# The input of two depthwise convolutions turned in 56-row tiles, with longer DMA runs

## The chip, the core and the metric

The kernel runs on one core of a Trainium2 chip. The metric is the device time of one execution in microseconds (us); the median of three runs counts.

## What is computed

A ConvNeXt block is followed by a second depthwise convolution, both in float32 over 16 images of 96 channels of 56x56 pixels.

```python
y = depthwise_conv7x7(x) + dw_b
y = layernorm_over_channels(y) * ln_w + ln_b
y = gelu(y @ w1 + b1)                                  # 96 -> 384
gx = sqrt(sum over pixels of y**2); nx = gx / (mean(gx) + 1e-6)
y = grn_gamma * (y * nx) + grn_beta + y
z = x + y @ w2 + b2                                    # 384 -> 96
out = depthwise_conv3x3(floor_to_2^-16(z), w_pow2) + bias_fixed
```

## The kernel before, in words

There are three stages, one after the other: the 7x7 convolution (`stages["a"]`, writes `y_scratch`), the two dense layers (writes `z_scratch`), and the 3x3 convolution (`stages["c"]`, writes the output). The change touches the two convolutions.

A convolution works on 24 batches of four channels (CB = 4), two batches to a loop body (parity p). Its contraction runs over 112 partitions, which are a pair of image rows (2 x 56 columns); weights are banded 112x128 tables, one set for each channel. For each batch the following happens, with `s` running over 0 to 3:

- SP loads the batch (`load_rows`, L341) into `xin`: 112 partitions are 2 images (even and odd) x 4 channels x 14 runs of four rows; in each partition lie 8 image pairs x 224 elements. Two DMAs of 56 partitions each. The tables follow (`load_tables`, L368).
- PE turns the input (`tin`, L593): each transpose takes 112 partitions x 112 elements (a row pair of 8 channel-images) and writes 112 partitions x 112 elements in PSUM. A group `s` is four transposes for four images; the two banks `p_in` alternate, so group n waits until group n-2 has been evicted. Groups of the next batch are turned ahead by the table `AHEAD`: groups 0 and 1 before channel 0, group 2 before channel 1, group 3 before channel 2.
- ACT copies each group to `xt_h` (rounded to fp32r, `xt_copy`, L745, two instructions of 112x224) and DVE makes the low part `xt_l` (`low_part`, L951, two instructions of 112x224).
- PE convolves channel `s` (`convolve`, L617): 12 matmuls of 464 columns in the 7x7 stage, 4 in the 3x3 stage, into one of two banks `p_conv`. It first waits until the channel two before has been evicted.
- The result is copied to `yt` in three instructions of 224 elements (`yt_copy`): ACT (L762) does it for all channels of the 7x7 stage and for channels 0 to 2 of the 3x3 stage, DVE (L1155) for channel 3 of the 3x3 stage.
- PE turns a quarter of the batch before back (`back`, L644): eight transposes of 56 partitions x 112 elements, alternately from the upper and the lower half of the partitions, each half into its own bank. The wait for the output buffer (`back_waits`) stands ahead of the last matmul of `convolve`.
- The turned rows are copied to `ost` by `out_copy`: ACT (L772) in the 7x7 stage, DVE (L1144) in the 3x3 stage. The 7x7 stage has one pair of banks for this (`p_back`), the 3x3 stage two pairs, which alternate. SP stores the batch in two DMAs of 56 partitions (L385), two batches later in the 7x7 stage and three in the 3x3 stage.

Each engine runs its list in the written order. On DVE in the 3x3 stage this is, for each `s`: `low_part` of the groups turned ahead, then at `s` = 3 the copy `yt_copy`, then `out_copy` of the batch before. In the 7x7 stage DVE runs `low_part` and then three instructions of the running mean and variance (`update`); ACT runs `xt_copy` with `table_high` (L780), then `yt_copy`, then `out_copy`.

## Time and profile before

| | |
|---|---|
| median of three runs | 1070.03 us (1067.22 to 1071.70) |
| profiled execution | 1071.91 us; its span 1070.1 us |
| PE busy | 992.1 us, 93% of the span |
| PE weight loads | 718.5 us, 67% |
| DVE busy | 822.0 us, 77% |
| ACT busy | 823.5 us, 77% |
| POOL busy | 415.4 us, 39% |
| DMA | 182.95 MB in 146788 packets, 140564 of them under 2 KB; mean 171 GB/s |

The 7x7 stage takes about the first 350 us, the dense layers run to about 870 us, the 3x3 stage takes the rest. Busy times of PE hold modelled ends of pipelined matmuls; starts are measured, so the cost of a group of PE instructions is read here from its start to the start of the next group.

### The profile page before, as it was taken

How to read it: one execution, taken by the hardware profiler on the slowest of the kernel's cores; microseconds unless marked ns; L12 is line 12 of the kernel's file. 1: busy time of each engine (PE TensorE's matmuls, PEld its weight loads, DVE VectorE, ACT ScalarE, POOL GpSimd, SP SyncE). 2: the span in 40 equal slices, each digit the busy share in tenths (PEclk: the TensorE clock that was granted, in tenths of full speed). 3: DMA queues.
4: the chain of work that ended last, by engine and by line, in shares of the span. 5: the costliest groups of instructions: out<-in, count | busy, mean ns of one | idle time of the engine just before them, and what ended most of it. 6: DMA issues, size and time to landing. Idle time of an engine off the chain costs nothing.

```text
span 1070.1 us, 21112 instructions
## 1 busy us (share of the span) xinstructions
PE 992.1 (93%) x5574; PEld 718.5 (67%) x5574; DVE 822.0 (77%) x1718; ACT 823.5 (77%) x1715; POOL 415.4 (39%) x357
## 2 busy tenths in 40 slices
PE   5999999999999378999999999999999869999996
PEld 4788888888888265666666666666666427777774
DVE  5777777777777567988888888888887767888885
ACT  3688888888887356789898888888888608787874
POOL 3576766766766145333233323333332001111110
PEclk9899999999999667999999999999999989999998
DMA  8377777777774492555555555555543347999995
GB/s 183 99 189 183 183 181 180 180 182 180 181 180 120 126 235 76 179 155 177 164 172 161 177 164 171 162 169 163 165 141 90 101 116 178 244 251 243 249 240 150
DMA packets 146788, 182.95 MB, mean 171 GB/s; under 512 B 13939, under 2 KB 140564, under 8 KB 143796
## 3 DMA queue, kind: packets, MB, share of 16 engines
q1 hardware_dynamic: 144020, 179.86, 62.8%
q10 hardware_dynamic: 2736, 2.72, 1.2%
q8 instruction: 13, 0.21, 0.1%
q14 instruction: 19, 0.16, 0.1%
HBM read 124.28 MB, written 58.25 MB: 171 GB/s over the span
## 4 chain that ended last, share of the span: by engine, by line
PE 70%; DVE 10%; ACT 7%; issue 5%; DMA 4%; SPq 1%; DVEq 1%; POOL 1%; ACTq 0%; POOLq 0%
PE psum L617 21%; PE psum L697 21%; PE psum L687 6%; PE psum L688 6%; PE psum L689 6%; PE psum L593 5%; PE psum L644 3%; DVE arena_r L951 3%; ACT arena L762 3%; ACT arena_r L745 2%; DVE arena L979 1%; DVE arena L975 1%; DMA arena<-lines_a 1%; ACT arena L850 1%; DVE arena L1155 1%
## 5 line engine op out<-in xcount | busy, mean ns | idle before, releaser
L617 PE MATMUL psum<-arena_r 112*128 112x464 f32 x1536 | 375.9, 386 | 3.5 <-DVE arena_r L951 3.3
L617 PEld LDWEIGHTS psum<-arena_r 112*128 112x128 f32 x1536 | 277.1, 190 | 36.7 <-issue 3.0
L697 PE MATMUL psum<-arena,w2s 128*96 128x448 f32 x672 | 269.2, 545 | 5.8 <-DVE psum L1072 3.0
L850 ACT ACTIVATE arena<-psum,b1g 128x448 f32<-128x448 f32 x336 | 201.7, 631 | 60.2 <-PE psum L689 60.2
L528 POOL TENSOR_TENSOR arena_r<-arena,arena_r 96x448 fp32r<-96x448 f32 x112 | 136.9, 1222 | 268.8 <-DVE arena_r L1025 212.2
L697 PEld LDWEIGHTS psum<-arena,w2s 128*96 128x96 f32 x672 | 110.4, 165 | 124.4 <-issue 112.9
L687 PE MATMUL psum<-arena_r,w1h 96*128 96x448 f32 x336 | 153.8, 458 | 16.1 <-POOL arena_r L528 16.1
L762 ACT ACTIVATE arena<-psum,bias_a 64x224 f32<-64x224 f32 (+1 forms) x288 | 117.3, 443 | 59.0 <-PE psum L617 48.9
L951 DVE TENSOR_TENSOR arena_r<-psum,arena_r 112x224 fp32r<-112x224 f32 x384 | 127.4, 382 | 42.9 <-ACT arena_r L745 42.2
L517 POOL TENSOR_TENSOR arena<-arena 128x448 f32<-128x448 f32 x96 | 110.3, 1149 | 111.6 <-DVE arena L979 111.0
L745 ACT ACTIVATE arena_r<-psum 112x224 fp32r<-112x224 f32 x384 | 112.7, 356 | 52.9 <-PE psum L593 51.6
L817 ACT ACTIVATE arena<-arena 128x1792 bf16<-128x1792 f32 (+1 forms) x91 | 136.8, 1503 | 2.7
L593 PE MATMUL psum<-ident,arena 112*112 112x112 f32 x768 | 107.5, 274 | 28.2 <-DVE arena_r L951 13.1
L502 POOL TENSOR_TENSOR arena_r<-arena,arena_r 112x512 fp32r<-112x512 f32 x96 | 123.2, 1297 | 15.2 <-ACT arena_r L780 15.2
L688 PE MATMUL psum<-arena_r,w1h 96*128 96x448 f32 x336 | 126.2, 376 | 0.0
L689 PE MATMUL psum<-arena_r,w1l 96*128 96x448 f32 x336 | 125.8, 375 | 0.0
L975 DVE TENSOR_TENSOR arena<-arena,psum 128x448 f32<-128x448 f32 x96 | 59.6, 621 | 82.7 <-ACT arena L762 82.7
L593 PEld LDWEIGHTS psum<-ident,arena 112*112 112x112 f32 x768 | 76.7, 137 | 41.9 <-DVE arena_r L951 21.6
L762 ACT ACTIVATE arena<-psum,bias_c 64x224 f32<-64x224 f32 (+1 forms) x216 | 88.1, 442 | 18.2 <-PE psum L617 16.4
L644 PEld LDWEIGHTS psum<-ident,arena 56*112 56x112 f32 x1536 | 57.5, 131 | 62.7 <-issue 57.7
L1072 DVE TENSOR_TENSOR psum<-arena,psum 96x448 f32<-96x448 f32 x112 | 69.6, 621 | 33.3 <-PE psum L697 32.9
L559 POOL CAST arena_r<-arena 112x1024 fp32r<-112x1024 bf16 x24 | 25.0, 1042 | 175.8 <-PE psum L617 159.9
(98 smaller groups left out, 1145.5 us busy)
## 6 DMA issues: line engine op xcount, KB each, us to landing
arena<-lines_a SPq DMA_DIRECT2D x46, 448.0 KB
arena<-in_x_dram SPq DMA_DIRECT2D x48, 392.0 KB
y_scratch<-arena SPq DMA_DIRECT2D x48, 392.0 KB
arena<-in_x_dram SPq DMA_DIRECT2D x112, 168.0 KB, 2.6
z_scratch<-arena SPq DMA_DIRECT2D x112, 168.0 KB, 2.0
out_dram<-arena SPq DMA_DIRECT2D x48, 392.0 KB
arena<-z_scratch SPq DMA_DIRECT2D x44, 392.0 KB
arena_r<-y_scratch SPq DMA_DIRECT2D x98, 168.0 KB, 2.6
```

The costliest lines, as they stand in the source:

```text
L528: pool.tensor_tensor(yl[:, CH * t:CH * t + CH], ct[:, (t + p) % 2, :], yh[:, CH * t:CH * t + CH].bitcast(F32), ALU.subtract).then_inc(yn_r ...
L593: mm = nc.tensor.transpose(p_in[s % 2][0:PAIR, at:at + CM], xin[:, p, IG // 2 * s + i, PAIR * h:PAIR * h + PAIR], ident[0:CM, 0:CM])
L617: mm = nc.tensor.matmul(p_conv[s % 2][:, 0:NCOL], w[:, p, s, TW * k:TW * k + TW], v[:, p, s, slot0 + k:slot0 + k + JP, :].rearrange("p j i ...
L687: nc.tensor.matmul(p_h[m][:, 0:CH], w1h[:, w], yh[:, cols], start=True, stop=False)
L688: nc.tensor.matmul(p_h[m][:, 0:CH], w1h[:, w], yl[:, cols], start=False, stop=False)
L689: nc.tensor.matmul(p_h[m][:, 0:CH], w1l[:, w], yh[:, cols], start=False, stop=True).then_inc(h_done, 1)
L697: mm = nc.tensor.matmul(p_o[k][0:C, 0:CH], w2s[:, p, m, :], hid[p][:, m, CH * t:CH * t + CH], start=(m == 0), stop=(m == MT - 1))
L745: ins = nc.scalar.activation(tile_group(xt_h, p, s, h), bank_group(s, h), ACT.Identity)
L762: ins = nc.scalar.activation(to[part, q], cols[part, :, :, j:j + 2 * NRUN - 1:2], ACT.Identity, bias=bias[part, bass.ds(n, 1)], scale=scale)
L817: nc.scalar.activation(sqd[:, 0:CH * (t1 - t0)], hid[p][:, m, CH * t0:CH * t1], ACT.Square, accum_out=ss[:, p, m, part:part + 1]).then_inc ...
L850: nc.scalar.activation(hid[p][:, m, CH * t:CH * t + CH], p_h[m][:, 0:CH], ACT.Gelu, bias=b1g[:, m:m + 1]).then_inc(gelu_done, 1)
L951: ins = dve.tensor_tensor(tile_group(xt_l, p, s, h), bank_group(s, h), tile_group(xt_h, p, s, h).bitcast(F32), ALU.subtract)
```

## The change

Rows are loaded and stored in runs of eight instead of four (RUN = 448 elements, 7 runs to an image). Four images instead of two lie in the partitions: on the load side two in partitions 0 to 55 and two in 64 to 119 (images of the first and of the second eight), on the store side all four in 0 to 111. A load or store of a batch is four DMAs of 28 partitions instead of two of 56; the bytes are the same and each contiguous piece is twice as long.

The input is turned in two halves `u` of a batch instead of four groups. A half is 16 transposes of 56 partitions x 112 elements, alternately from the lower and the upper half of the array, each into its own bank, so a half fills a pair of banks. `TURN` puts half 0 ahead of channel 0 and half 1 ahead of channel 2. The 7x7 stage has one such pair (`p_in["a"]`; its first batch also borrows the banks of `p_conv`), the 3x3 stage two. For this the 3x3 stage gives up the second pair of `p_back`: both stages now have one. The waits of `tin` are moved ahead of the last matmul of the convolution before it. `xt_copy` and `low_part` are four instructions for each half of a batch, still of 224 elements, and signal after every two.

The copy to `yt` is one instruction of 336 elements on 128 partitions and two of 112 on 64 partitions, instead of three of 224. `yt` has another order of pixels, with runs of 7 instead of 14 elements. The number of transposes back, their shape and the copies out of them stay as they were.

```diff
-RUN = 4 * W
-NRUN = H // 4
+RUN = 8 * W
+NRUN = H // 8
+RP = 4
-CM = 2 * CR
+CM = 4 * CR
+HM = 2 * CR
+TURN = ((0,), (), (1,), ())
+TURN0 = ((), (0,), (), (1,))
-        p_in, p_conv = bank[0:2], bank[2:4]
-        p_back = {"a": [psum[:, 4:6, :]], "c": [psum[:, 4:6, :], psum[:, 6:8, :]]}
+        p_conv, p_back = bank[2:4], psum[:, 4:6, :]
+        p_in = {"a": [psum[:, 0:2, :]], "c": [psum[:, 0:2, :], psum[:, 6:8, :]]}
...
+        def turned_back(s, p):
+            to = yt[:, p].rearrange("p q i (c m) -> p q c i m", c=CB)[:, :, s]
...
+            return ((to[:, 1:RP], odd[:, 0:RP - 1], slice(0, TW)), (to[low, 0], even[low, 0], low), (to[high, 0], odd[high, RP - 1], high))
...
-                for g in range(2):
-                    sp.dma_start(xin[CR * g:CR * g + CR, s, :, :], rows_of[g][bass.ds(b * CR, CR)]).then_inc(S[f"x{s}"], 16)
+                for g in range(4):
+                    sp.dma_start(xin[in_part(g), s, :, :], image_rows(src, g)[bass.ds(b * CR, CR)]).then_inc(S[f"x{s}"], 16)
...
-                    need(pe, S["xt"], n - 1)
-                    for h in range(2):
-                        for i in range(IG // 2):
-                            at = CM * (IG // 2 * h + i)
-                            mm = nc.tensor.transpose(p_in[s % 2][0:PAIR, at:at + CM],
-                                                     xin[:, p, IG // 2 * s + i, PAIR * h:PAIR * h + PAIR], ident[0:CM, 0:CM])
+                    need(pe, S["xt"], 4 * b + 2 * u - 2 * (len(p_in["a" if S is stages["a"] else "c"]) - 1))
...
+                    for h in range(RP):
+                        for i in range(2):
+                            at = HM * (2 * h + i)
+                            for half in range(2):
+                                q = LSTEP * half
+                                mm = nc.tensor.transpose(in_pair(S, b, u)[0:PAIR, half, at:at + HM],
+                                                         xin[q:q + HM, p, 2 * u + i, PAIR * h:PAIR * h + PAIR],
+                                                         ident[q:q + HM, q:q + HM])
...
-                        if then_back and n == len(todo) - 1:
-                            back_waits(b - 1, s)
+                        if n == len(todo) - 1:
+                            if then_back:
+                                back_waits(b - 1, s)
+                            for q in then_turn:
+                                tin_waits(*q)
...
-                    need(pe, S["out"], G * b + s + 1 - len(outs))
+                    need(pe, S["out"], G * b + s)
...
-                dve.tensor_copy(rows_group(p, s), forwards(p_back["c"][s % 2][0:CM], IG)).then_inc(S["out"], 1)
+                dve.tensor_copy(rows_group(p, s), forwards(p_back[0:CM], RP)).then_inc(S["out"], 1)
```

Ahead of the 3x3 stage the first two batches are loaded in two steps: what has been written of z so far, and then the last two images (`first_rows`). Before, three of the four groups to be turned rested on the first step alone; now one of the two halves does.

## Rows read from the trace of the kernel before

**Rows 1.** Windows: us, busy PE PEld DVE ACT POOL, clock, DMA share, GB/s.

```profile
200.00:300.00 100.00, 99.29 (x693) 81.34 (x692) 73.76 (x145) 81.64 (x201) 69.34 (x59) 1.00 0.73 182
600.00:840.00 240.00, 240.00 (x889) 155.94 (x888) 197.96 (x410) 212.98 (x334) 72.70 (x61) 1.00 0.51 152
950.00:1000.00 50.00, 47.43 (x432) 35.44 (x430) 40.96 (x101) 40.57 (x116) 6.55 (x7) 1.00 0.94 247
```

**Rows 2.** Timeline, PE in the 7x7 stage: start us, us, line, shapes.

```profile
203.67 0.43 PE L644 MATMUL psum<-ident,arena 56*112 56x56 f32 x8
204.03 0.98 PE L593 MATMUL psum<-ident,arena 112*112 112x112 f32 x8
204.78 2.77 PE L617 MATMUL psum<-arena_r 112*128 112x464 f32 x12
207.48 0.43 PE L644 MATMUL psum<-ident,arena 56*112 56x56 f32 x8
208.01 0.60 PE L593 MATMUL psum<-ident,arena 112*112 112x112 f32 x4
208.37 2.76 PE L617 MATMUL psum<-arena_r 112*128 112x464 f32 x12
```

**Rows 3.** Lines, the whole span: two copies out of PSUM on ACT.

```profile
L762 ACT ACTIVATE arena<-psum,bias_a 64x224 f32<-64x224 f32 (+1 forms) x288 | 117.3, 443 | 59.0 <-PE psum L617 48.9 <-DVE arena L979 8.8
...
L772 ACT ACTIVATE arena<-psum 112x448 f32<-112x448 f32 x96 | 52.5, 546 | 5.1 <-PE psum L644 2.9
```

**Rows 4.** Timeline, all engines, one batch of the 3x3 stage.

```profile
942.65 1.10 ACT L745 ACTIVATE arena_r<-psum 112x224 fp32r<-112x224 f32 x4 [0.88 <-PE psum L593]
...
942.68 1.09 PE L617 MATMUL psum<-arena_r 112*128 112x464 f32 x4
943.10 0.62 DVE L1144 COPY arena<-psum 112x448 f32<-112x448 f32 x1
...
943.70 0.42 PE L644 MATMUL psum<-ident,arena 56*112 56x56 f32 x8
943.75 1.28 DVE L951 TENSOR_TENSOR arena_r<-psum,arena_r 112x224 fp32r<-112x224 f32 x4
...
944.50 0.59 PE L593 MATMUL psum<-ident,arena 112*112 112x112 f32 x4 [0.37 <-DVE arena_r L951]
...
944.96 0.61 DVE L1144 COPY arena<-psum 112x448 f32<-112x448 f32 x1
...
947.05 1.36 SPq L341 DMA_DIRECT2D arena<-z_scratch  x2
...
949.01 0.42 PE L644 MATMUL psum<-ident,arena 56*112 56x56 f32 x8
949.24 1.27 DVE L1155 TENSOR_SCALAR arena<-psum,bias_c 128x224 f32<-128x224 f32 x3
```

**Rows 5.** Waits, the whole span (us in total, times, longest).

```profile
PE psum L593 <- DVE arena_r L951: 13.1, 25, 2.9
...
PE psum L593 <- DMA arena<-z_scratch: 3.1, 1, 3.1
```

**Rows 6.** DMA issues, the whole span.

```profile
out_dram<-arena SPq DMA_DIRECT2D x48, 392.0 KB
...
arena<-lines_c SPq DMA_DIRECT2D x48, 112.0 KB
```

**Rows 7.** Timeline, all engines, the last channels and the tail.

```profile
1056.50 0.42 PE L644 MATMUL psum<-ident,arena 56*112 56x56 f32 x8
...
1056.97 0.62 DVE L1144 COPY arena<-psum 112x448 f32<-112x448 f32 x1 [0.78 <-PE psum L644]
...
1061.40 0.96 PE L644 MATMUL psum<-ident,arena 56*112 56x56 f32 x16 [0.18 <-DVE arena L1144]
```

**Rows 8.** Windows: two half microseconds of the tail, stores alone.

```profile
1063.50:1064.00 0.50, 0.00 (x0) 0.00 (x0) 0.14 (x1) 0.00 (x0) 0.00 (x0) 0.58 0.82 168
...
1066.00:1066.50 0.50, 0.00 (x0) 0.00 (x0) 0.00 (x0) 0.00 (x0) 0.00 (x0) 0.50 0.96 326
```

More of the change, by code:

```diff
@@ L470, in _ @@
             for b in range(2):
-                first_rows(b, 0, NI2 - 1, c_early[b])
+                for g in range(4):
+                    first_rows(b, g, 0, NI - g // 2, c_early[b])
                 tables_c(b, b)
@@ L657, in body @@
                         for s in range(G):
+                            turns = TURN0 if first and p == 0 else TURN
                             if not (last and p == 1):
-                                for q in (AHEAD0 if first and p == 0 else AHEAD)[s]:
-                                    tin(b + 1, q, 1 - p)
-                            convolve(b, s, p, not (first and p == 0))
+                                for u in turns[s]:
+                                    tin(b + 1, u, 1 - p)
+                            then_turn = [(b + 1, u, 1 - p) for u in turns[s + 1]] if s + 1 < G else [(b + 2, u, p) for u in TURN[0]]
+                            if last and (p == 1 or s + 1 == G):
+                                then_turn = []
+                            convolve(b, s, p, not (first and p == 0), then_turn)
                             if not (first and p == 0):
@@ L736, in conv_stage, with xt_copy @@
             def conv_stage(S, bias, scale, rows_too):
-                def xt_copy(b, s, p):
-                    act.wait_ge(S["tin"], G * b + s + 1)
-                    if s == 0:
+                def xt_copy(b, u, p):
+                    act.wait_ge(S["tin"], 2 * b + u + 1)
+                    if u == 0:
                         need(act, S["conv"], CB * (b - 1))
-                    for h in range(2):
-                        ins = nc.scalar.activation(tile_group(xt_h, p, s, h), bank_group(s, h), ACT.Identity)
-                    ins.then_inc(S["xh"], 1)
+                    for half in range(2):
+                        for c in range(2):
+                            ins = nc.scalar.activation(turned(xt_h, p, u, half, c), in_bank(S, b, u, half, c), ACT.Identity)
+                        ins.then_inc(S["xh"], 1)
                 def yt_copy(b, s, p):
@@ L780, in table_high @@
                     nc.scalar.activation(toep_h[:, p, s, :], toep[:, p, s, :], ACT.Identity).then_inc(S["th"], 1)
-                for s in range(G):
-                    if rows_too and s == G - 1:
+                for u in range(2):
+                    if rows_too and u == 1:
                         table_high(0, 0, 0)
-                    xt_copy(0, s, 0)
+                    xt_copy(0, u, 0)
                 if rows_too:
@@ L963, in body @@
                             if not (last and p == 1):
-                                for q in (AHEAD0 if first and p == 0 else AHEAD)[s]:
-                                    low_part(S, b + 1, q, 1 - p)
+                                for u in (TURN0 if first and p == 0 else TURN)[s]:
+                                    low_part(S, b + 1, u, 1 - p)
                             update(b, s, p)
```

155 lines of the change are left out of this document (78 added, 77 removed).

## The prediction, made before the changed kernel was run

> **What bounds the kernel now.** The windows come first [rows 1]: in the 7x7 stage PE is busy 99.29 of 100 us, in the dense layers all the time (the change leaves these alone), in the 3x3 stage 47.43 of 50 us, there with the DMA engines busy 0.94 of the time. So the question in the first stage is what a turn costs on PE, in the third whether PE, DVE or the DMA sets the pace.
>
> The timelines answer it. In the 7x7 stage, start to start [rows 2]: eight 56x56 transposes back 0.36 us (203.67 to 204.03), eight 112x112 turns 0.75 (to 204.78), four turns 0.36, a channel of 12 matmuls 2.70 (to 207.48). The turn at 208.01 starts 0.17 later than 207.48 + 0.36. In the 3x3 stage [rows 4] a channel takes 1.02 us (942.68 to 943.70), the transposes back 0.36, and the turn at 944.50 starts 0.44 late, named as waiting for DVE. One batch is 2x0.36 + 0.75 = 1.47 of turns, 4x1.02 = 4.08 of matmuls, 4x0.36 = 1.44 of transposes back and 0.44 of wait: 7.43 us. So nothing but DVE holds PE in a batch. The waits agree [rows 5]: turns waited 13.1 us for L951, and for a DMA of z only once, 3.1 us.
>
> **Turns.** The new form, 56x112 with 56 moving columns, is the form of L644: 0.36 us for eight [rows 2], so 0.72 for a half of 16 and 1.44 for a batch, against 1.47. A pair in both halves of the array turns what one 112x112 tile turned and takes 0.09 us against 0.09. The turns themselves give 0.03 us a batch. The Trainium skill (TensorEngine Tiling (Array Packing), Theoretical Speedup) promises up to twice the speed where a dimension is at most 64; by that a half would cost 0.36. The row speaks against it, since L644 is already tiled so; it is a rival below.
>
> **7x7 stage.** The wait of 0.17 goes, as the pair has two channels (over 6 us) to be evicted. ACT then has, ahead of channel 0, four copies (1.10, [rows 4]), two tables of 512 columns (estimate 0.62 each, from L772's 546 ns for 448), 1.15 to `yt` and 0.55 out [rows 3], about 4.0 us against a slot of 3.78; the next slot has 1.1 us less work than it lasts, and the bank is not wanted again for over 2 us. So no wait follows. Gain: 0.20 a batch x 23 = -4.6. At the start both halves are turned without waiting for an eviction: estimate -1 (between 0 and -2).
>
> **Copy to `yt`.** Three of 224 become 336 + 112 + 112. From L762 (224: 443 ns) and L772 (448: 546 ns) [rows 3] a column costs between 0.46 ns (their difference, over 224 columns) and 1.4 (DVE's 0.62 us for 448, with nothing fixed [rows 4]). 112 columns fewer are 0.05 to 0.15 us; I take 0.1, so 1.15 for both engines. The shorter runs are not in the trace; bound: 0 to +10%.
>
> **3x3 stage: the second pair of output banks.** This is the term that decides. `back` of slot s may now start only when `out_copy` of s-1 has ended on DVE, and DVE runs `low_part` ahead of it. The hand over from PE to DVE takes 0.05 (1056.50 + 0.42 to 1056.97) and from DVE to PE 0.06 (1061.34 to 1061.40) [rows 7]; DVE's `yt` copy begins 0.23 after the `back` behind its channel (949.01 to 949.24); the last matmul of a channel starts 0.78 after the first, 0.24 ahead of `back` (four matmuls in 1.02). Durations [rows 4]: `out_copy` 0.62, four `low_part` 1.21 (943.75 to 944.96), the first two 0.61, ACT's four copies 1.10, of which I take the first two to be done at 0.61 (half, and the end of one). I lay out one batch, time 0 at its first turn, in steady state (the batch before ended with `back` 3 at -0.36):
>
> - DVE: `yt` of channel 3 from -0.13 to 1.02, `out_copy` 3 to 1.64. The last matmul of channel 0 would start at 0.72 + 0.78 = 1.50 and waits to 1.69: **0.19**. `back` 0 at 1.94.
> - ACT has the first half's copies at 1.45 and 1.94. DVE runs `low_part` 1.64 to 2.85, `out_copy` 0 to 3.47. The last matmul of channel 1 is due at 1.94 + 0.36 + 0.78 = 3.08 and waits to 3.52: **0.44**. `back` 1 at 3.76.
> - Turn from 4.12 to 4.84. ACT is in `yt` 1 until 5.14, so its first two copies are done at 5.75. DVE: `out_copy` 1 from 4.23 to 4.85 (in time for channel 2, `back` 2 at 5.86), `low_part` 5.78 to 6.99, `out_copy` 2 to 7.61. The last matmul of channel 3 is due at 5.86 + 0.36 + 0.78 = 7.00 and waits to 7.66: **0.66**. `back` 3 at 7.90, next batch at 8.26.
>
> Without waits the batch is 1.44 + 4.08 + 1.44 = 6.96; with 1.29 of waits 8.25, against 7.43: +0.82 x 22 batches with turns and transposes back (1 to 22) = **+18.0**. The wait at the turn is gone (the two pairs of `p_in`), yet what it bought is smaller than what the banks cost. Bounds: no wait at all is 6.96, -0.47 x 22 = -10; all copies 10% longer lengthen the chain by some 0.3, +25.
>
> **DMAs.** Twice as many are issued: SP needs 0.68 for each load by 1.36 for two [rows 4], at most 2.7 a batch, with four stores at most as long and 0.9 for tables, 6.3 of 8.25 us. A load is issued at 947.05 and turned from two batches after 941.93, at 956.8, so 1.4 us more of issue lies under 9.7 of lead. Pieces of 1792 bytes move in the dense layers at 152 / 0.51 = 298 GB/s for each unit of busy share, those of 896 here at 247 / 0.94 = 263 [rows 1]; nothing waits for either, so 0.
>
> **Edges.** Into the 3x3 stage half the turns, not a quarter, wait for the last images: one more copy and `low_part` pair, about +0.9, of which channel 1's eviction order gives half back: +0.4. At the end the four last transposes back go one for one with DVE: each 0.47 + 0.62 + 0.06 = 1.15 instead of 0.62, +2.1 at the last copy; the last store then has the queue to itself, so I take +0.7.
>
> **Sum.** -4.6 - 1.0 + 18.0 + 0.4 + 0.7 = +13.5. The profiled span goes from 1070.1 to 1083.6 (execution 1071.9 to 1085.4, it stands 1.9 above the median). Against the median 1070.0: **1083.5 us**.
>
> **Rivals.**
> - *DVE keeps its dates*, the waits of 1.29 don't arise (6.96 a batch): 1070 - 4.5 - 10.3 = 1055. Against it: DVE's order is written out, and its copies alone fill 6.2 of 7.4 us. 0.07.
> - *Paired turns cost half* (0.36 for 16): 0.72 less a batch in both stages, 1083.5 - 0.72x(23 + 22) = 1051. Speaks for it only the rule above, against it L644. 0.04.
> - *The DMA bound the 3x3 stage*: pieces at 298 instead of 263 GB/s take 12% off 7.43, 0.88 x 22 = -19, so 1070 - 4.5 - 19 = 1046. The share 0.94 speaks for it; the named waits against. 0.03.
> - *Slower stores and loads*: the tail has stores alone at 168 GB/s and at 326 [rows 8], so nearly the same busy share can mean half the rate. A batch moves 1.84 MB (four DMAs of 392 KB and two of 112, KB of 1024 bytes [rows 6]). With the stores alone at 168 and the rest at 326 it needs 4.8 + 3.2 = 8.0 us, no loss yet; from 222 GB/s for all (8.25 us) it decides, and at 168 it is 10.9 us and 1083.5 + 2.7x22 = 1142. Against it: both rates belong to the same transfers. 0.05. The Trainium skill (SBUF — State Buffer, Door 1: The DMA port swizzle) says that the rate hangs on how many of 16 ports the partitions reach: 28 reach 7, the 56 from 0 on reach 8. No run here shows ports.
> - *Shorter waits*, 0.88 instead of 1.29 in a batch (slack that I don't see): +9 instead of +18, 1074.5, within 0.5%. 0.06.
>
> **How the numbers follow.** The forecast holds 0.75, from 1077 (each of the three waits 0.1 shorter) to 1095 (copies 10% longer, and the rest of the bounds). The range 1072 to 1095 takes in the last rival and leaves the others out. Half a per cent, 5.4 us, is about what a measurement can tell from no change: faster 0.14 (three rivals), same 0.06, slower 0.80 (forecast and slow transfers). Outside the 3x3 batches the terms are -4.5; a batch of 7.43 + 4.5/22 = 7.63, so 0.67 us of waits, is the point from which the change loses.
>
> **What would show it.** 56x112 turns of 0.72 for 16; a 7x7 batch of some 13.7 us; in the 3x3 stage 8.2 to 8.3 us a batch with PE waiting for L1144's copy inside channels 1 and 3, not at turns; DMA share lower than 0.94. A batch near 7.0, or turns of 0.4, would make me wrong; PE waiting for DMAs of z would show the fourth rival.

## The result, and the profile after

| | |
|---|---|
| median | 1107.9 us (the kernel before in the same runs: 1070.9) |
| ratio to before | 1.0333, 95% interval 1.0306 to 1.0361 |
| profiled execution | 1108.1 us; its span 1106.3 us (before 1070.1) |
| PE, weight loads, DVE, ACT busy | 91%, 64%, 75%, 73% of the span |
| DMA | 183.00 MB in 106471 packets |

Slower, as predicted, and by 37 us instead of 13.5. (One of the four executions took 1124.51 us at a granted clock of 0.902 instead of 0.94; the ratio leaves it out.) The windows of the changed kernel (columns as in [rows 1]):

```profile
200.00:300.00 100.00, 99.30 (x837) 79.89 (x836) 77.41 (x150) 81.71 (x207) 70.37 (x60) 1.00 0.78 186
950.00:1000.00 50.00, 41.98 (x443) 27.99 (x442) 33.36 (x83) 32.07 (x96) 5.21 (x5) 0.94 0.84 203
```

The 7x7 stage is as full as before. In the 3x3 stage every engine and the DMA have become idler than in [rows 1]: PE 41.98 instead of 47.43 us, DVE 33.36 instead of 40.96, ACT 32.07 instead of 40.57, DMA share 0.84 instead of 0.94. No resource is full, so the engines must be waiting for one another. The granted clock of that window is 0.94 instead of 1.00.

Where the time went, from the first and last turn of the 3x3 stage in each trace:

| part of the span | before | after | difference |
|---|---|---|---|
| up to the first turn of the 3x3 stage | 870.97 | 864.95 | -6.0 |
| from its first turn to its last | 179.49 | 217.51 | +38.0 |
| from the last turn to the end | 19.6 | 23.8 | +4.2 |

The first row compares one trace of each kernel. In another trace with the 7x7 stage of the kernel before, the 3x3 stage begins at 868.46 (the run with one output pair below); in three others with the 7x7 stage of the changed kernel, at 862.65 to 864.29. So the 6.0 stands for something between 3.5 and 8.3.

The timeline of PE in the 7x7 stage (columns as in [rows 2]):

```profile
208.12 0.47 PE L653 MATMUL psum<-arena_r 112*128 112x464 f32 x1 [0.23 <-ACT arena L803]
208.52 0.42 PE L677 MATMUL psum<-ident,arena 56*112 56x56 f32 x8
208.78 0.61 PE L625 MATMUL psum<-ident,arena 56*112 56x56 f32 x16
209.32 2.79 PE L653 MATMUL psum<-arena_r 112*128 112x464 f32 x12
212.04 0.43 PE L677 MATMUL psum<-ident,arena 56*112 56x56 f32 x8
212.40 2.77 PE L653 MATMUL psum<-arena_r 112*128 112x464 f32 x12
215.11 0.43 PE L677 MATMUL psum<-ident,arena 56*112 56x56 f32 x8
215.37 0.60 PE L625 MATMUL psum<-ident,arena 56*112 56x56 f32 x16
```

From start to start the 16 new turns take 0.54 us (208.78 to 209.32), and eight transposes back that stand directly ahead of them 0.26 (208.52 to 208.78) instead of the 0.36 of those ahead of matmuls (212.04 to 212.40). A half-batch, from turn to turn, takes 6.59 us (208.78 to 215.37). The first line is the other side of it: the last matmul of a channel waits for ACT's copy out, and it takes 0.40 to the transposes (208.12 to 208.52), where the prediction's unwaited one takes 0.24.

The timeline of PE, DVE and ACT in the 3x3 stage of the changed kernel, one batch and a bit, cut to the lines that set the pace:

```profile
962.33 0.60 PE L625 MATMUL psum<-ident,arena 56*112 56x56 f32 x16
...
965.33 0.62 DVE L1176 COPY arena<-psum 112x448 f32<-112x448 f32 x1
...
966.09 0.47 PE L653 MATMUL psum<-arena_r 112*128 112x464 f32 x1 [0.92 <-DVE arena L1176]
966.50 0.43 PE L677 MATMUL psum<-ident,arena 56*112 56x56 f32 x8
966.71 1.16 DVE L1184 TENSOR_SCALAR arena<-psum,bias_c 128x336 f32<-128x336 f32 x3 [0.77 <-PE psum L653]
966.76 0.61 PE L625 MATMUL psum<-ident,arena 56*112 56x56 f32 x16
...
967.51 1.10 ACT L782 ACTIVATE arena_r<-psum 112x224 fp32r<-112x224 f32 x4 [1.69 <-PE psum L625]
967.90 0.62 DVE L1176 COPY arena<-psum 112x448 f32<-112x448 f32 x1
968.56 1.28 DVE L983 TENSOR_TENSOR arena_r<-psum,arena_r 112x224 fp32r<-112x224 f32 x4
968.58 0.48 PE L653 MATMUL psum<-arena_r 112*128 112x464 f32 x1 [0.37 <-DVE arena L1176]
...
969.76 0.62 DVE L1176 COPY arena<-psum 112x448 f32<-112x448 f32 x1
970.51 0.47 PE L653 MATMUL psum<-arena_r 112*128 112x464 f32 x1 [0.26 <-DVE arena L1176]
971.11 1.21 ACT L796 ACTIVATE arena<-psum,bias_c 128x336 f32<-128x336 f32 x3 [0.70 <-PE psum L653]
971.17 0.61 PE L625 MATMUL psum<-ident,arena 56*112 56x56 f32 x16
972.34 1.10 ACT L782 ACTIVATE arena_r<-psum 112x224 fp32r<-112x224 f32 x4
972.97 1.28 DVE L983 TENSOR_TENSOR arena_r<-psum,arena_r 112x224 fp32r<-112x224 f32 x4 [0.97 <-ACT arena_r L782]
974.17 0.61 DVE L1176 COPY arena<-psum 112x448 f32<-112x448 f32 x1
975.06 0.47 PE L653 MATMUL psum<-arena_r 112*128 112x464 f32 x1 [1.04 <-DVE arena L1176]
```

A batch is 8.84 us (turns at 962.33 and 971.17), against 7.44 before. It is a closed circle: a chain over PE, DVE and ACT that ends at its own start one batch later. Each link starts when the one before ends:

- The last matmul of channel 3 (966.09) was held for the output pair. So its result comes late, and DVE, idle 0.77 us for it, copies channel 3 from 966.71.
- `out_copy` stands behind that on DVE (967.90), then `low_part` (968.56) and the next `out_copy` (969.76), for which the last matmul of channel 1 waits (970.51).
- So ACT, idle 0.70, copies channel 1 from 971.11, and the turned input only from 972.34.
- `low_part` waits for that (972.97), `out_copy` stands behind it (974.17), and the last matmul of channel 3 waits for that again (975.06).

Round once, 8.97 us here (966.09 to 975.06); the round ahead of it, from 957.31 to 966.09, is 8.78. The two alternate, mostly because from the end of `out_copy` to the last matmul of channel 3 it is 0.28 us here and 0.14 in the round ahead (965.95 to 966.09).

The waits in the 3x3 stage (880 to 1090 us: engine, line, waited for, us in total, times, longest) show the same three links, PE for the copy out, ACT and DVE for the channel:

```profile
ACT arena L796 <- PE psum L653: 39.6, 50, 3.1
...
PE psum L653 <- DVE arena L1176: 26.5, 43, 1.0
...
DVE arena L1184 <- PE psum L653: 19.8, 22, 1.3
```

### The profile page after: what moved, and what is told of

Same layout as the page of the kernel before. It is cut to its first block, busy times and chain, and to the rows that moved or that the text cites. A ratio compares the mean times of both kernels' runs of the same rounds, so it can differ in the third digit from the quotient of the medians.

```text
span 1106.3 us, 23147 instructions
## 1 busy us (share of the span) xinstructions
PE 1001.5 (91%) x6342; PEld 706.9 (64%) x6342; DVE 825.9 (75%) x1717; ACT 810.4 (73%) x1715; POOL 415.6 (38%) x357
## 2 busy tenths in 40 slices
DMA packets 106471, 183.00 MB, mean 165 GB/s; under 512 B 16627, under 2 KB 100244, under 8 KB 103476
## 4 chain that ended last, share of the span: by engine, by line
PE 67%; DVE 10%; DMA 7%; issue 6%; ACT 5%; SPq 3%; POOL 0%; DVEq 0%; ACTq 0%; POOLq 0%
PE psum L653 23%; PE psum L733 20%; PE psum L723 6%; PE psum L724 6%; PE psum L725 5%; PE psum L677 4%; DMA arena<-lines_a 3%; DVE arena_r L983 3%; DVE arena L1176 3%; PE psum L625 2%; ACT arena L796 2%; DVE arena L1184 1%; ACT arena_r L782 1%; DMA arena_r<-y_scratch 1%; SPq L413 1%
## 5 line engine op out<-in xcount | busy, mean ns | idle before, releaser
L653 PE MATMUL psum<-arena_r 112*128 112x464 f32 x1536 | 412.7, 405 | 39.1 <-DVE arena L1176 26.5
L653 PEld LDWEIGHTS psum<-arena_r 112*128 112x128 f32 x1536 | 287.0, 197 | 106.8 <-DVE arena_r L983 25.6
L782 ACT ACTIVATE arena_r<-psum 112x224 fp32r<-112x224 f32 x384 | 104.9, 363 | 71.5 <-PE psum L625 70.8
L796 ACT ACTIVATE arena<-psum,bias_a 64x112 f32<-64x112 f32 (+1 forms) x288 | 111.0, 423 | 55.8 <-PE psum L653 44.4
L983 DVE TENSOR_TENSOR arena_r<-psum,arena_r 112x224 fp32r<-112x224 f32 x384 | 122.9, 382 | 35.4 <-ACT arena_r L782 34.5
L796 ACT ACTIVATE arena<-psum,bias_c 64x112 f32<-64x112 f32 (+1 forms) x216 | 84.1, 428 | 44.7 <-PE psum L653 43.3
L677 PEld LDWEIGHTS psum<-ident,arena 56*112 56x112 f32 x1536 | 60.3, 138 | 63.6 <-issue 57.0
L677 PE MATMUL psum<-ident,arena 56*112 56x56 f32 x1536 | 86.2, 235 | 7.2 <-DVE arena L1176 3.8
L723 PEld LDWEIGHTS psum<-arena_r,w1h 96*128 96x128 f32 x336 | 65.6, 195 | 38.5 <-POOL arena_r L556 18.4
```

Source lines behind the costliest of these rows:

```text
L653: mm = nc.tensor.matmul(p_conv[s % 2][:, 0:NCOL], w[:, p, s, TW * k:TW * k + TW], v[:, p, s, slot0 + k:slot0 + k + JP, :].rearrange("p j i ...
L677: mm = nc.tensor.transpose(p_back[0:CM, 1 - r, W * h:W * h + W], rows, ident[q:q + W, q:q + W])
L723: nc.tensor.matmul(p_h[m][:, 0:CH], w1h[:, w], yh[:, cols], start=True, stop=False)
L796: ins = nc.scalar.activation(to, cols, ACT.Identity, bias=bias[part, bass.ds(n, 1)], scale=scale)
L983: ins = dve.tensor_tensor(turned(xt_l, p, u, half, c), in_bank(S, b, u, half, c), turned(xt_h, p, u, half, c).bitcast(F32), ALU.subtract)
```

## The experiments

An edit moves the line numbers below it by up to ten: L658 of one kernel is the L653 of the changed one. The measured time is a median, the ratio is that to the kernel before in the same runs, "stage" is the time from the first turn to the last of the 3x3 stage (179.5 us before, 217.5 after).

### Two output pairs again

```diff
-        p_conv, p_back = bank[2:4], psum[:, 4:6, :]
-        p_in = {"a": [psum[:, 0:2, :]], "c": [psum[:, 0:2, :], psum[:, 6:8, :]]}
+        p_conv = bank[2:4]
+        p_back = {"a": [psum[:, 4:6, :]], "c": [psum[:, 4:6, :], psum[:, 6:8, :]]}
+        p_in = {"a": [psum[:, 0:2, :]], "c": [psum[:, 0:2, :]]}
...
```

The transposes back and DVE's `out_copy` alternate between the two pairs, and the wait for the pair is for the copy two back. The 3x3 stage pays with one of its two pairs for turns.

> The changed kernel with, in the 3x3 stage, two pairs of output banks that alternate (as before the change) and one pair of input banks. Theory A (the single output pair, which ties every transpose back to DVE's last copy, makes the 3x3 batch 8.8 us long where it was 7.4, and the gaps let the clock fall): the waits for the output copy ahead of the last matmul go, a batch takes PE's own 6.4 us and some wait for the evicted input, 7.0 at most, the granted clock stays 1.0, total about 1057 us. Theory B (transfers over 28 partitions move fewer bytes for the same busy share, 203 GB/s at 0.84 against 247 at 0.94, and bound the stage next): 1.84 MB at 242 GB/s are 7.6 us a batch, the DMA share near 1.0, total about 1070. Theory C (the order of DMAs and waits on SP and PE is the cause, not the banks): stays near 1105.

Measured: 1073.38 us, ratio 1.0031 (1.0017 to 1.0045), stage 186.8 us, 7.62 a batch. Nearly the whole loss hangs on the output pair. The time is near Theory B's, not the 1057 of Theory A. But the DMA share is 0.90, not near 1.0, and two runs below take B out as the reason for the 7.62 (1074.46 and 1058.3 us). The clock of the window is back, and most of the DMA share:

```profile
950.00:1000.00 50.00, 47.27 (x523) 31.31 (x523) 38.98 (x98) 37.81 (x113) 6.27 (x6) 1.00 0.90 242
```

### DVE copies out first

```diff
+                            if S is stages["c"]:
+                                update(b, s, p)
                             if not (last and p == 1):
                                 for u in (TURN0 if first and p == 0 else TURN)[s]:
                                     low_part(S, b + 1, u, 1 - p)
-                            update(b, s, p)
+                            if S is stages["a"]:
+                                update(b, s, p)
```

> The changed kernel with one edit on DVE in the 3x3 stage: the copy of the finished rows out of PSUM stands ahead of the four low-part instructions of the same slot, not behind them. Theory A: the wait in channel 1 (0.5 us) and the one in channel 3 (1.2 us) lose the 1.2 us of low parts that stood before them, a batch takes about 7.3 us, between 7.0 and 7.6, and the whole 1070 us with less or no loss of clock. Theory B: the same or somewhat slower, limited at 7.6 us a batch, 1073. Theory C: no change from 1108.

Measured: 1088.62 us, ratio 1.0164 (1.0124 to 1.0203), stage 197.3 us, half-batches of 4.4 to 4.6 and 3.5 to 3.6 us in turn. DVE's written order is one link of the circle; taking it out gives back half. That lies between the 1070 to 1073 of Theories A and B and the 1108 of C.

### The kernel before with one output pair

```diff
-        p_back = {"a": [psum[:, 4:6, :]], "c": [psum[:, 4:6, :], psum[:, 6:8, :]]}
+        p_back = {"a": [psum[:, 4:6, :]], "c": [psum[:, 4:6, :]]}
...
```

> The kernel before with one edit: the 3x3 stage has one pair of output banks instead of two. Theory A: PE waits for DVE's output copy in each channel that has low parts ahead of it on DVE, 0.4 to 0.8 us each and 0.17 more for each wait because the weights of the matmul that waits are not loaded ahead: a batch 8.4 to 8.9 us instead of 7.44, and the clock falls in places, 1092 to 1110 us. Theories B and C: within 3 us of the kernel before.

Measured: 1096.32 us, ratio 1.0243 (1.0212 to 1.0275), 8.38 a batch at the full clock. The pair alone, with the old turns and the old transfers, costs 26 us, as Theory A had it. Both waits of the convolution for DVE's copy out are there, that of the weight load and that of the matmul (the waits of PEld and of PE, whole span):

```profile
PEld psum L617 <- DVE arena L1144: 31.5, 74, 0.7
...
PE psum L617 <- DVE arena L1144: 11.1, 42, 0.9
```

### The kernel before with transfers of 28 partitions

```diff
-                    sp.dma_start(xin[CR * g:CR * g + CR, s, :, :], rows_of[g][bass.ds(b * CR, CR)]).then_inc(S[f"x{s}"], 16)
+                    for r in range(2):
+                        q = CR // 2 * r
+                        sp.dma_start(xin[CR * g + q:CR * g + q + CR // 2, s, :, :], rows_of[g][bass.ds(b * CR + q, CR // 2)]).then_inc(S[f"x{s}"], 16)
```

(and the same for the stores, with the counts of the waits doubled)

> The kernel before with one edit: each load and each store of a batch is cut in two, so that four DMAs of 28 partitions move what two of 56 moved; pieces stay at 896 bytes. Theory A: at most 5 us slower, from tables that land later in the 7x7 stage. Theory B: the 3x3 stage, where the DMA share is 0.94 already, becomes bound by its transfers: 8 us a batch or more, and the whole 1085 us or more.

Measured: 1074.46 us, ratio 1.0041 (1.0020 to 1.0061), 7.44 a batch as before, stage 179.9 us:

```profile
950.00:1000.00 50.00, 47.47 (x430) 35.41 (x429) 40.98 (x101) 40.54 (x116) 6.34 (x7) 1.00 0.95 244
```

Twice as many transfers of half the partitions run at 244 GB/s and a share of 0.95; 247 and 0.94 in [rows 1]. The stage doesn't notice, and Theory B's 1085 is out. So the rival of slow transfers is out as the cause, and so is the number of DMA issues.

### PE kept busy with redundant matmuls

```diff
+                    if S is stages["c"] and then_back:
+                        for _ in range((1, 1, 0, 3)[s]):
+                            k, w, v = todo[0]
+                            nc.tensor.matmul(p_conv[s % 2][:, 0:NCOL], w[:, p, s, TW * k:TW * k + TW],
+                                             v[:, p, s, slot0 + k:slot0 + k + JP, :].rearrange("p j i -> p (j i)"),
+                                             start=True, stop=True)
```

> The changed kernel with five more matmuls in each batch of the 3x3 stage: the first matmul of channels 0 and 1 is issued once more, that of channel 3 three times more (same operands, so the result is the same). They lie ahead of the waits for DVE, which last 0.67, 0.54 and 1.22 us in these channels, against 0.25 us for a matmul. Theory A1 (the waits lengthen the batch, and besides they leave PE idle enough for the granted clock to fall to half in stretches of 10 to 17 us, about 9 us in all): the batch stays 8.8 us, the granted clock stays at 1.0 in the stage, total 1098 to 1101 us. Theory A2 (the clock falls for another reason, or its fall costs nothing since DVE sets the pace): 1106 to 1112.

Measured: 1099.07 us, ratio 1.0283 (1.0251 to 1.0316), 8.84 a batch, unchanged, stage 209.6 us. In the changed kernel the granted clock falls in stretches of the stage, in this one it doesn't. First the changed kernel, then the one with the filler:

```profile
985.00:1000.00 15.00, 12.87 (x127) 8.63 (x122) 9.79 (x25) 9.27 (x28) 1.58 (x2) 0.84 0.84 203
1000.00:1015.00 15.00, 14.92 (x121) 10.50 (x121) 8.71 (x22) 7.82 (x24) 1.61 (x2) 0.59 0.69 160
1015.00:1030.00 15.00, 12.83 (x136) 8.50 (x135) 10.21 (x26) 10.28 (x32) 1.51 (x2) 1.00 0.85 210
```

```profile
880.00:1050.00 170.00, 158.02 (x1610) 109.24 (x1611) 115.00 (x288) 109.37 (x328) 19.80 (x19) 0.99 0.84 203
```

PE does more work and the kernel is 8.8 us faster: that much of the 37 is the clock. It follows from the gaps on PE and is no cause of the 8.84, which is the same at the full clock. The clock stands at 0.50 from 996 to 1012 us, the lower of the two levels (1.2 and 2.4 GHz), and half-batches there take up to 5.5 instead of 4.4 us; ahead of it, from 980 to 995 us, PE was busy 12.31 us at the full clock, with no gap over 1.1 us. From 905 to 920 us it was busy 12.31 us too and kept its clock, so the share alone doesn't tell when the clock falls. The Trainium skill (TensorE: Matmul & The Clock Gate, Part 1) says that the chip sets PE's clock by how busy PE has been, and by that rule redundant work can pay. The two kernels agree: in the window from 950 to 1000 us it is 0.94 with PE busy 41.98 us, and 1.00 with the filler and 46.55.

### Both waits behind the last matmul

```diff
-                        if n == len(todo) - 1:
-                            if then_back:
-                                back_waits(b - 1, s)
-                            for q in then_turn:
-                                tin_waits(*q)
...
                             if not (first and p == 0):
+                                back_waits(b - 1, s)
+                                pe.sem_inc(turn_go, 1)
                                 back(b - 1, s, 1 - p)
+                            for q in then_turn:
+                                tin_waits(*q)
+                            if then_turn:
+                                pe.sem_inc(turn_go, 1)
```

The waits are unchanged; each stands on a small instruction of its own ahead of the transposes that need it.

> The changed kernel with PE's waits for the output banks and for the next turn moved from ahead of the last matmul to behind it, each on an instruction of its own that only counts up a semaphore. Theory A1 (a matmul that waits starts its weight load only after the wait: 0.41 us from its start to the transposes behind it, against 0.25 in a row, three times a batch): the channel's result is ready before the wait ends, but the transposes now start without their loads; a batch shorter by 0.3 to 0.6 us of 8.84, total 1095 to 1102. Rival: the same loss moves to the transposes, batch within 0.1 us, 1105 to 1111.

Measured: 1069.54 us, ratio 1.000 (0.997 to 1.003), stage 182.6 us, 7.4 to 7.8 a batch. With one output pair and the new turns, the kernel is as fast as before. This was far more than expected, and moved the question from the number of banks to the place of the wait.

The 3x3 stage alone is still 3.1 us longer than before (182.6 against 179.5). The 7x7 stage, which has one output pair in all kernels, gains by the same edit: its last turn starts at 321.93 us, in the changed kernel at 329.95, though ACT waits as long for tables (11.5 us against 9.9). The 42 half-batches behind the first five that took 7.3 us more than 6.58 each in the changed kernel take 2.2 more here. These are single traces, and the profiled execution (1064.83) is one of the shortest of ten.

### The 7x7 tables ahead of three of the four loads

```diff
-                            load_rows(S, src, b + 1, 1 - s)
-                            tables(b + 1, 1 - s)
+                            if S is stages["a"]:
+                                load_rows(S, src, b + 1, 1 - s, (0,))
+                                tables(b + 1, 1 - s)
+                                load_rows(S, src, b + 1, 1 - s, (1, 2, 3))
+                            else:
+                                load_rows(S, src, b + 1, 1 - s)
+                                tables(b + 1, 1 - s)
```

> The changed kernel with the tables of a 7x7 batch issued behind the first of the four loads, not behind all four. In the changed kernel ACT waited 11.0 us for tables (16 times), and half-batches of the 7x7 stage took 6.9 to 8.2 us where undisturbed ones take 6.58, some 7 us in all. If the later tables are the cause (ACT late, its output copies late, PE waits for them), 4 to 7 us come back, total 1101 to 1104; if not, 1107 to 1110.

Measured: 1203.26 us, ratio 1.1256. The expectation was wrong: now the rows come late, where before ACT had only now and then waited for a table.

```profile
PE psum L658 <- DMA arena<-in_x_dram: 59.1, 21, 4.7
```

SP's order of the 7x7 stage has no slack for 448 KB of tables ahead of the rows; the late halves of that stage can't be mended there. (Most of them went with the moved waits of the experiment before.) It says nothing on the 3x3 stage.

### Two output pairs, the turns' wait behind, and the tables' order

> The kernel with two pairs of output banks in the 3x3 stage (1073.4 us, 7.62 us a batch, held by the wait for the low parts ahead of the last matmul) with two more edits: the waits of the turns stand behind the transposes back, on an instruction of their own, and the 7x7 tables are issued behind the first load. If the matmul that waits is what costs, a batch takes 7.0 to 7.3 us and the 7x7 stage gains 4 to 7 us: 1057 to 1062, faster than both kernels. If DVE's own 6.2 us of work with its hand-overs holds the batch at 7.6, only the tables count: 1067 to 1070.

The edit is the sum of the first experiment, of the last four added lines of the sixth, and of the one just told. Measured: 1118.15 us, ratio 1.0422, all of it lost in the 7x7 stage by the tables' order (its 3x3 stage begins at 923.8 us). The 3x3 stage takes 176.2 us, mostly 3.2 to 4.6 a half-batch, 10.6 less than with two pairs alone. So the run is a miss as a kernel and a hint for the next.

### Two output pairs, the turns' wait behind

The edit is the one just told without the tables' order: two output pairs and one pair for turns in the 3x3 stage, and in both stages the turns' waits behind the transposes back, on an instruction of their own.

> The changed kernel with two output pairs and one input pair in the 3x3 stage (as the run with two output pairs, 1073.4 us, 7.62 a batch) and PE's waits for the bank of the coming turns moved from the channel's last matmul to an instruction of their own behind the turns back, in both stages. Theory that a wait ahead of the last matmul delays the channel's result, and with it the waiter's own release: the 3x3 batch falls to 7.0 (the half-batches of 3.28 and 3.7 of the run that had this and a changed order of the tables), 0.6 x 22 = 13 below the run with two output pairs, and the 7x7 stage runs at 6.6 a half-batch: 1056 to 1062. Rival, that the wait costs the same wherever PE takes it (the time until the pair is free is the same): 1073. Rival, that the transfers bound the stage at this speed (DMA share 0.91 at 242 GB/s with 7.44 a batch): batch not under 7.2, 1064 to 1068.

Measured: 1058.3 us, ratio 0.9901 (0.9875 to 0.9928): faster than both kernels. Stage 170.2 us, 7.01 a batch. Against the kernel with two output pairs (1073.38) the place of the turns' wait alone is worth 15 us.

```profile
950.00:1000.00 50.00, 47.54 (x563) 34.06 (x561) 42.06 (x107) 40.19 (x121) 7.59 (x8) 1.00 0.93 262
```

262 GB/s at a share of 0.93, 15 more than the kernel before had in [rows 1]: the transfers, whose share of 0.94 looked like a limit there, had more to give. The median lies 6 us above the profiled execution (1051.95), which is the shortest of eleven, so the trace shows the kernel at its best.

### One wait moved at a time

The sixth experiment again, first with the turns' waits alone moved, then with the output pair's alone.

> The changed kernel; only PE's waits for the input bank of the coming turns go behind the turns back, on an instruction of their own; the wait for the output pair stays ahead of the last matmul. With both moved the kernel took 1069.5. In the 3x3 stage the waits of the last matmul were recorded as waits for DVE's out copy (43 times, 1.0 us), not for the turned copies. Theory that the output pair's wait carries the loss: 3x3 batch stays at 8.6 to 8.8, 1098 to 1106. Rival, that it is the turns' wait: 1070 to 1076. If both share it: about 1088.

Measured: 1101.77 us, ratio 1.0288 (1.0262 to 1.0315), stage 213.7 us, 8.7 a batch.

> The changed kernel; only PE's wait for the output pair goes behind the last matmul, on an instruction of its own ahead of the turns back; the turns' waits stay ahead of the last matmul. Theory that the output pair's wait carries the loss: 3x3 batch 7.4 to 7.8 and 1070 to 1080. Rival, that it is the turns' wait: 8.6 or more a batch, 1098 to 1106. If both share it: about 1088.

Measured: 1066.45 us, ratio 0.9963 (0.9946 to 0.9980), stage 178.3 us, 7.3 and 7.6 a batch in turn, somewhat less than expected. The output pair's wait carries the loss: moved alone it gives back 41 us, the turns' wait alone 6, and both together (1069.5) no more than the first. Some of the 41 is the clock, which is 1.00 from 880 to 1040 us here and falls in the changed kernel; against that kernel with the filler (1099.07) it is 33. PE waits for the copy out as often as after, 49 times against 43, for 18.2 us instead of 26.5. What is gone are DVE's waits for the channel, and most of ACT's. The waits of this kernel in the 3x3 stage:

```profile
PE psum L676 <- DVE arena L1177: 18.2, 49, 1.6
ACT arena L797 <- PE psum L652: 8.1, 26, 1.8
```

And its timeline where PE waits:

```profile
963.01 0.61 DVE L1177 COPY arena<-psum 112x448 f32<-112x448 f32 x1
963.54 1.16 DVE L1185 TENSOR_SCALAR arena<-psum,bias_c 128x336 f32<-128x336 f32 x3
...
963.76 0.43 PE L676 MATMUL psum<-ident,arena 56*112 56x56 f32 x8 [0.37 <-DVE arena L1177]
```

ACT waits 8.1 us for channels instead of 39.6. DVE's copy of channel 3 starts at 963.54 without idle time, ahead of the transposes that wait, where after it starts 0.77 late behind them. The circle is open at that link.

### The kernel before, the wait behind

> The kernel before, with PE's wait for the output pair moved behind the channel's last matmul, on an instruction of its own, in both stages; its turns already wait for themselves. With two output pairs in the 3x3 stage the pair is rarely the last to come there, so little is to be had: batch 7.3 to 7.44, 1066 to 1071. The 7x7 stage has one pair; PE's wait ahead of its last matmul was on DVE's low part and seldom on the pair. Rival, that the place of the wait is worth something at any number of pairs: 7.0 a batch in the 3x3 stage, 1058 to 1062. A loss, if the extra instruction costs more than it hides: 0.05 to 0.1 a channel, 92 + 92 channels, 1078 to 1085.

Measured: 1069.85 us, ratio 0.9992 (0.9978 to 1.0007), stage 180.9 us. With two output pairs the wait is not met there, and its place is worth nothing. This also gives the price of the extra instructions behind the last matmul: none that can be measured.

### The wait on its own instruction, ahead

The changed kernel with one added line:

```diff
                             if then_back:
                                 back_waits(b - 1, s)
+                                pe.sem_inc(turn_go, 1)
```

> The changed kernel; PE's wait for the output pair stays ahead of the channel's last matmul, but on an instruction of its own. Behind the last matmul the same instruction gave 1066.5 us; the wait on the matmul itself gave 1107.9. Theory of the place (the last matmul waits, so the channel's result comes late, the copy of it on DVE or ACT waits, and the out copy behind that copy too): the loss stays, 3x3 batch 8.6 to 8.9 and 1095 to 1108; the copies' waits for the convolution stay at about 40 us on ACT and 20 on DVE. Rival, that it was the wait on a matmul (weights loaded only after it, 0.17 us each, and what follows from that): 1066 to 1075. In between, 1080 to 1090, if both count.

Measured: 1121.65 us, ratio 1.0476 (1.0451 to 1.0502), stage 228.0 us. The same added instruction and the same wait as in the run with 1066.45 us, ahead of the last matmul instead of behind it: 55 us between the two. A part of it is the clock, 0.84 from 880 to 1040 us against 1.00; at the full clock the batches are 9.0 and 9.3 us in turn, against 7.3 and 7.6. The expectation (1095 to 1108) had the right theory and was too low. The waits of ACT and DVE for the channel are as long as after (3x3 stage):

```profile
ACT arena L798 <- PE psum L655: 43.9, 52, 1.5
...
DVE arena L1186 <- PE psum L655: 22.1, 21, 1.3
```

It is slower than the changed kernel too. The instruction lies in the circle: from the end of DVE's copy (950.97 + 0.61) to the last matmul are 0.30 us (951.88) instead of 0.14. The batch is longer by some 0.27 us, 6 us in 22 batches. The rest of the 13.75 was not separated; the granted clock from 880 to 1040 us is lower too, 0.84 against 0.88.

```profile
950.97 0.61 DVE L1178 COPY arena<-psum 112x448 f32<-112x448 f32 x1
...
951.88 0.47 PE L655 MATMUL psum<-arena_r 112*128 112x464 f32 x1 [1.07 <-DVE arena L1178]
952.29 0.43 PE L679 MATMUL psum<-ident,arena 56*112 56x56 f32 x8
```

What this doesn't separate: the weights of the last matmul are loaded behind the wait in either form (0.41 us from 951.88 to 952.29), so the late load and the late result are moved together.

### The kernel before with one output pair, the wait behind

The kernel before with the edits of the third experiment and of the one with 1069.85 us.

> The kernel before with one output pair in the 3x3 stage (1096.3 us, 8.38 a batch), and PE's wait for the pair moved behind the last matmul, on an instruction of its own. Theory of the place: it returns most of the 26 us, batch 7.4 to 7.7 and 1070 to 1078. Rival, that the pair is late by itself in that kernel, since its turns and its copies fill the engines (unwaited batch 7.0 against 6.4 of the changed kernel): batch 8.0 to 8.4, 1086 to 1097.

Measured: 1075.40 us, ratio 1.0056 (1.0040 to 1.0071), stage 183.3 us, 7.56 and 7.75 a batch in turn. The lost pair costs 5 us instead of 26, with the turns and transfers of before. So the finding doesn't hang on the new turns.

## Why the prediction was right and wrong

**Right: the sign, the stage and the cause.** The gain up to the 3x3 stage was forecast at 5.6, and 6.0 came, by luck (see the turns below); the 3x3 stage decides, PE waits for L1176 inside the channels and not at turns, the DMA share falls below 0.94. With two output pairs the loss is gone (1073.4), with one pair in the kernel before it is there (1096.3).

**Wrong: the term of the 3x3 batch, +0.82 forecast and +1.40 measured.** 22 x 1.40 is 30.8 us instead of 18.0. The layout had the right waits in the right order, of 0.19, 0.44 and 0.66, and its chain from the last matmul of channel 3 to the same one a batch later is the circle of the trace. It priced this circle at 8.25. In the trace they are 0.67, 0.54 and 1.22, counting what the last matmul is late against 0.78 after the first and what it then takes above 0.24. PE's unwaited part is 6.41 instead of 6.96, and this gained nothing, since the circle over DVE and ACT has its own length. A batch, the mean of two rounds, is some 0.6 us longer than laid out:

- A held matmul takes 0.41 to the transposes instead of 0.24 (966.09 to 966.50), and the copy of the channel starts 0.62 after it (966.09 to 966.71; 970.51 to 971.11 on ACT is 0.60) where I had 0.47. That link is met twice in a round: +0.28.
- From DVE's end to PE's matmul I took the 0.06 of a handover in the tail [rows 7]. In the circle it is 0.13 ahead of channel 1's last matmul (970.38 to 970.51), and ahead of channel 3's 0.14 and 0.23 to 0.28 in turn (965.95 to 966.09, 974.78 to 975.06): +0.15 to +0.29.
- The channel's copy takes 1.19 and 1.23 to the next instruction (966.71 to 967.90, 971.11 to 972.34) instead of 1.15: +0.12. Its guess was from columns alone.

Together that is 0.55 to 0.69, so the three cover it. The step that failed is the handover costs: each was taken from the nearest row, but from a row in which PE did not hold a channel back, and none of the three in a form that occurs in the circle. The bound of +25 allowed for copies 10% longer and for no longer handover.

**Left out: the clock.** The stage at 8.84 a batch leaves PE idle enough to lose its clock in stretches; 8 to 9 us (stage 217.5 against 209.6, time 1107.9 against 1099.1, with the filler). The prediction had no term for it, though it forecast 1.29 us of waits in 8.25.

The span became 36.2 us longer instead of 13.5. Of the 22.7 us between, the batch has 12.8, the clock about 8 and the end 3.5 (below); that leaves about -1.6 for the 7x7 stage and the start of the 3x3 stage. For this start the prediction had +0.4; from the first turn to that of the second batch it is 12.28 us instead of 11.65.

**The turns: wrong row, compensated.** Of the 16 turns I said 0.72 from L644's eight in 0.36. In a row they take 0.54. The 0.36 of eight holds about 0.1 for the change to the matmuls that follow; eight of them alone ahead of the turns take 0.26, so 24 in a row take 0.80, 0.033 each. A 7x7 batch without waits is 13.17 us instead of 13.89: -0.72 instead of -0.20, about -16 in all. It didn't arrive: 42 half-batches, all behind the first five, together are 7.3 us above 6.58 each, and at least a part of it is the last matmul waiting for ACT's copy out (the line at 208.12; 5 such waits have 3.0 us), which the prediction had said would not happen. The waits of ACT in the 7x7 stage (30 to 345 us) show what makes it late there, tables that land late (3.7 us before):

```profile
ACT arena_r L811 <- DMA arena<-lines_a: 9.9, 15, 1.9
```

The tables alone don't cost the time: with both waits behind the last matmul ACT waits for them 11.5 us, and the stage's last turn comes 8 us earlier. What is left, some 2 us, lies at the start. The term of -5.6 was met by luck: a gain of 16 where it had 4.6, and losses where it had none. The rival "paired turns cost half" (0.36 for 16) is wrong as stated, but was nearer than I allowed: the turns cost three quarters. The Trainium skill (TensorEngine Tiling (Array Packing), Theoretical Speedup) promises up to twice; the row shows 0.54 against the 0.75 of eight full tiles ahead of matmuls.

**The end.** +0.7 forecast, +4.2 measured. From the last turn to the end of the last channel it is 11.1 us instead of 8.9: two channels wait 0.74 and 0.82 us for DVE's copy out, and the three behind them take 1.55 us each with their transposes instead of 1.40, since the weights of each last matmul are held for that copy. The timeline of PE there:

```profile
1090.44 0.43 PE L677 MATMUL psum<-ident,arena 56*112 56x56 f32 x8
1090.80 1.27 PE L653 MATMUL psum<-arena_r 112*128 112x464 f32 x4
1092.00 0.43 PE L677 MATMUL psum<-ident,arena 56*112 56x56 f32 x8
...
1097.91 0.62 PE L677 MATMUL psum<-ident,arena 56*112 56x56 f32 x8 [0.72 <-DVE arena L1176]
```

From there to the end of the transposes back it is 2.7 more, where I had 2.1 (the last two groups take 0.62 at a granted clock of 0.50), and the stores behind give 0.7 back, where I had 1.4. The step left out is the channels ahead of the tail.

**The rivals.** Slower transfers: out (1074.46 and an unchanged batch with transfers of 28 partitions). The DMA bound: out (262 GB/s are reached). Paired turns at half the cost: out as stated, told above. Shorter waits: out, they were longer. DVE keeps its dates: out, but it is the one that a wait in the right place comes near to; 1055 was its price, and 1058.3 is the kernel with two output pairs and the turns' wait behind the last matmul.

**What the change cost itself.** What decides is the loss of the output pair together with something that the change left as it was: the wait of `back` ahead of the last matmul. With two pairs it cost nothing there (1069.85 with it moved); with one pair it costs nearly all. The prediction took its place as given and had no rival for it. The waits of `tin`, which the change moved to the same place, cost 6 us with one output pair (1101.77 with them behind) and 15 with two. With two output pairs and the turns' wait behind, the change wins: 1058.3 us against 1070. How much of that is the new turns and how much the longer pieces of the transfers was not tested.

**Open.** How the 33 us that the place of the wait is worth beside the clock divide between the late result and the late weights of the held matmul. The fastest kernel's runs scatter from 1052 to 1071 us, and with them the mean granted clock of the execution (0.964 at 1051.95, 0.946 at 1071.26); why it differs between executions is open.

## What to carry to other kernels

A wait that is met belongs behind the last instruction whose result others wait for, even at the price of an instruction of its own: ahead of it, it holds back the very engines that will release it, and a missing buffer becomes a circle. Before a buffer is given up, lay out that circle as a loop over all engines, with its handovers, and take its length and not PE's as the time of a batch; work saved on PE gains nothing inside it. If such a loop leaves gaps on PE, price the clock too.

## What the runs showed of the hardware

- 56x112 transposes in alternating halves of the array take 0.033 us each in a row of 24 (208.52 to 209.32), and eight of them ahead of 112-row matmuls 0.045.
- A matmul that is held by a wait takes 0.38 to 0.41 us to the next instruction instead of 0.24. It starts 0.05 to 0.28 us after the end of the copy that it waits for, most often 0.13 to 0.15; 0.28 to 0.30 in the same places, and up to 0.40, with the wait on a separate instruction ahead.
- The granted clock was 0.50 for 16 us (996 to 1012) behind 15 us in which PE was busy 12.31 us with no gap over 1.1 us, and 0.99 over 170 us with five redundant matmuls a batch.
- Transfers of 28 partitions reached 262 GB/s at a share of 0.93, and in the kernel before they left the rate about where it was (244 GB/s at 0.95 against 247 at 0.94). By the Trainium skill (SBUF — State Buffer, Door 1: The DMA port swizzle) the bandwidth hangs on how many of the 16 ports the partitions reach, and by its table 28 partitions reach 7 and 56 reach 8. The runs show little of that, 257 instead of 263 GB/s for each unit of busy share.
